# A two-layer decoder on one core: new order of the turn, with a ring of 12 decays

## What is computed

```python
x = ln(x + rfs(x) @ weights.T)                 # 1 random features: exp(x@proj - |x|^2/2 ...)
x = ln(x + xattn(x, ctx, ctx))                 # 2 cross attention, 16 heads of 16, 120 keys
x = ln(x + coupling(x))                        # 3 three cycles of a 4-layer gelu network and a rotation
x = ln(x + mamba(x))                           # 4 below
x = ln(x + gated(x, ctx, ctx, ctx))            # 5 gelu(x@ctx.T) * (x@ctx.T) @ ctx
x = ln(x + moe(x))                             # 6 router, 8 experts, the best one weighted by its gate

def coupling(x):                               # 3
    g = global_net(x.mean(rows)); out = x
    for _ in range(3):
        t = sigmoid(w4 @ gelu(w3 @ gelu(w2 @ gelu(w1 @ out))))
        out = out + (0.1 + range * (0.7*g + 0.3*t - 0.5) * 2) * twist(out)
    return out

def mamba(x):                                  # 4
    xs, res = split(x @ W_in.T)                # 512 + 512 columns
    xc = silu(conv4(xs) + b)
    delta = softplus(xc)
    for n in range(16):                        # 16 states per column
        h[n] = scan(h[n] * exp(-delta * exp(A_log[n])) + xc*xc)
    return ((sum(h) * silu(res) + D) * xc) @ W_out.T
```

## Time and profile before

| | |
|---|---|
| device time, median of 3 runs | 3486.57 us |
| the profiled execution: its time, its span | 3486.94 us, 3485.1 us |
| mean granted TensorE clock | 0.814 of full |
| PE, PE weight load busy | 76%, 43% of the span |
| DVE busy | 76% |
| ACT, POOL busy | 45%, 46% |
| DMA | 13 GB/s mean |

### The profile page before, as it was taken

One profiled execution on the slowest core, in us unless ns is written; L12 is line 12 of the kernel. 1 busy time (PEld: TensorE's weight loads), 2 busy tenths in 40 slices (PEclk: granted clock), 3 DMA queues, 4 the chain that ended last, 5 costly groups with the idle time before them and its releaser, 6 DMA issues.

```text
span 3485.1 us, 41835 instructions
## 1 busy us (share of the span) xinstructions
PE 2634.2 (76%) x10956; PEld 1505.0 (43%) x10956; DVE 2650.8 (76%) x4314; ACT 1564.4 (45%) x2838; POOL 1610.6 (46%) x1223
## 2 busy tenths in 40 slices
PE   5876878787786887768787786877778787777746
PEld 3434435354443544435354443544445353443413
DVE  2287887968789687887968789696877968788693
ACT  1364544535345453544535445453544545354430
POOL 1064461735537263562735437262562726447180
PEclk8868788887888878888887888888788887888877
DMA  3000000000000000000000000000000000000000
GB/s 115 0 16 0 21 1 27 0 22 6 0 27 0 27 0 7 21 0 27 0 22 6 0 27 0 27 0 13 15 0 27 0 22 6 0 12 0 12 0 12
DMA packets 16786, 45.63 MB, mean 13 GB/s; under 512 B 2376, under 2 KB 6992, under 8 KB 16336
## 3 DMA queue, kind: packets, MB, share of 16 engines
q1 hardware_dynamic: 16592, 43.90, 3.5%
HBM read 35.50 MB, written 8.39 MB: 13 GB/s over the span
## 4 chain that ended last, share of the span: by engine, by line
PE 37%; DVE 28%; issue 19%; ACT 9%; POOL 4%; DVEq 2%; SPq 0%; DMA 0%; ACTq 0%; POOLq 0%
PE bank L487 35%; DVE h_ring L1010 10%; POOL ysum L1537 4%; DVE x L392 3%; DVE x L1107 2%; PE bank L400 2%; DVE smax L915 2%; DVE soft L990 2%; ACT a_ring L1372 1%; DVE ln_stats L374 1%; DVE xpad L1016 1%; ACT soft L1349 1%; DVE qT L965 1%; ACT bank L1367 1%; ACT kmask L1312 1%
## 5 line engine op out<-in xcount | busy, mean ns | idle before, releaser
L1537 POOL TENSOR_TENSOR ysum<-ysum,h_ring 128x512 f32<-128x512 f32 x896 | 1152.4, 1286 | 476.5 <-DVE h_ring L1010 411.2
L1010 DVE TENSOR_TENSOR_SCAN h_ring<-a_ring,bank 128x512 f32<-128x512 f32 x1024 | 1170.9, 1199 | 103.2 <-ACT a_ring L1372 50.8
L487 PE MATMUL bank<-w_expert_w,x45T 128*128 128x512 f32 x1024 | 607.8, 732 | 226.2 <-DVE x L1107 224.6
L1372 ACT ACTIVATE a_ring<-soft,decay 128x510 f32<-128x510 f32 x1024 | 666.7, 715 | 141.7 <-DVE h_ring L1010 140.2
L1513 POOL TENSOR_TENSOR kmask<-kT,w_columns 128x960 f32<-128x960 f32 x64 | 115.5, 1838 | 753.8 <-ACT kT L1260 753.8
L487 PEld LDWEIGHTS bank<-w_expert_w,x45T 128*128 128x128 f32 x1024 | 212.3, 224 | 501.4 <-DVE x L1107 276.2
L1282 ACT ACTIVATE probs<-bank 120x512 f32<-120x512 f32 x256 | 138.3, 593 | 411.8 <-PE bank L487 411.8
L487 PE MATMUL bank<-kmask,w_cn_w 128*128 128x256 f32 (+2 forms) x768 | 277.3, 470 | 44.1 <-ACT kmask L1316 20.3
L400 PE MATMUL bank<-w_ident,x 128*128 128x128 f32 x640 | 136.8, 350 | 224.9 <-DVE x L392 224.9
L1107 DVE SCALAR_TENSOR_TENSOR x<-bank,weight,x 128x256 f32<-128x256 f32 x512 | 212.0, 471 | 72.0 <-PE bank L487 72.0
L962 DVE TENSOR_SCALAR kmask<-kmask,gate_scale,base 128x256 f32<-128x256 f32 x96 | 40.3, 420 | 278.7 <-ACT kmask L1326 278.7
(11 more groups left out here) (144 smaller groups left out, 3879.8 us busy)
## 6 DMA issues: line engine op xcount, KB each, us to landing
x0T<-in_xT SPq DMA_DIRECT2D x16, 512.0 KB, 3.2
x<-in_x SPq DMA_DIRECT2D x16, 512.0 KB, 4.2
out<-x SPq DMA_DIRECT2D x16, 512.0 KB, 3.1
ctxT<-in_ctxT SPq DMA_DIRECT2D x16, 240.0 KB, 4.3
ctxTb<-in_ctxT SPq DMA_DIRECT2D x16, 240.0 KB, 2.6
ctxb<-in_ctx SPq DMA_DIRECT2D x16, 240.0 KB, 3.1
w_expert_w<-in_expert_w SPq DMA_DIRECT2D x1, 2048.0 KB
w_winT<-in_winT SPq DMA_DIRECT2D x1, 1024.0 KB
```

The source lines that it names most:

```text
L487: return pe.matmul(o, l, r, start=start, stop=stop)
L1010: scanned.then(v.tensor_tensor_scan(h_ring[:, k % HRING, :], a_ring[:, k % RING, :, :].rearrange("p b s -> p (b s)"), xc2, 0.0, ALU.mult, ...
L1372: a.activation(a_ring[:, k % RING, :, 1:S], delta[:, c, :].rearrange("p (b s) -> p b s", b=NB)[:, :, 1:S], ACT.Exp, scale=decay[:, k:k + 1 ...
L1537: p.tensor_tensor(out=total, in0=first, in1=h_ring[:, k % HRING, :], op=ALU.add)\
```

## The change

The computation is the same. What changes is the order of a turn and what goes with it:

- RING is 12. `BEFORE_COUPLING` is step 54 of the plan, after scan 51. All steps from there (12 scans and an out) are done on DVE between the rotations, two scans per cycle; the last out follows the cycles. ACT still ends all decays before the first gelu of the cycles, so that decay 63 waits for scan 51. On DVE all 54 steps, and then `global_base`, stand ahead of the scans that are left.
- The output projection of m (`mamba_out`) and its layer norm (`ln4_sum`) move out of the cycles into the head of the next turn, where the group is b. ACT keeps a copy of its residual (`keep`).
- `mamba_in` 0 to 3 moves up in the head, before the projection of f; `mamba_in` 4 to 7 moves out of the head to between the attention's scores, all into bank 4, each waiting for ACT to have read the one before. ACT loads the silu table once more for it.
- `convolve`, silu and softplus are cut in halves, and DVE does the norm of f between them.
- Keys and values of the next group are made in cycles 1 and 2. Keys are masked by ACT (4 activations with a scale of 0 or 1 per partition); POOL's `mask_keys` is gone, and tiles that lay in kmask get their own memory.
- `combine` and `experts` steps, maxima and the softmax steps of ACT get new places: expert 13 comes after the transposes of norm 2 on PE, experts 14 and 15 in cycles 1 and 2.
- POOL squares the next group's input (`norms`) before its additions of chunk 3.

```diff
-RING = 8
+RING = 12
+BEFORE_COUPLING = AFTER["scan", (IC * STATES - RING - 1) // STATES, (IC * STATES - RING - 1) % STATES]
...
 # PE, turn
                 if b is not None:
-                    norm_turn(pe, n4, b, MB)
+                    mamba_out(b, 0, 8)
+                if m is not None:
+                    norm_turn(pe, n3, m, TURN)
+                if b is not None:
+                    mamba_out(b, 8, 16)
+                if m is not None:
+                    mamba_in(m, f, 0, IC)
...
                     project(f, n1, feats_ready, feats, rf_out, DC, OUT12)
                 if b is not None:
+                    norm_turn(pe, n4, b, MB)
                     gated_in(b)
...
+                    norm_turn(pe, n1, f, TURN)
+                    queries(f)
+                    scores(f, 0, 2)
+                if b is not None:
+                    gated_out(b)
+                if f is not None:
+                    scores(f, 2, 3)
+                if b is not None:
+                    norm_turn(pe, n5, b, MB)
+                if f is not None:
+                    scores(f, 3, 4)
+                if b is not None:
+                    router(b)
+                if f is not None:
+                    scores(f, 4, 5)
+                if b is not None:
+                    turn_weights(b)
                 if m is not None:
+                    mamba_in(m, f, IC, IC + 1)
                 if b is not None:
                     expert_bias(b)
+                for j in range(3):
+                    if f is not None:
+                        scores(f, 5 + j, 6 + j)
+                    if m is not None:
+                        mamba_in(m, f, IC + 1 + j, IC + 2 + j)
...
-                    experts(b, 12, 14)
+                    experts(b, 12, 13)
                 if f is not None:
                     norm_turn(pe, n2, f, TURN)
                 if b is not None:
-                    experts(b, 14, 15)
+                    experts(b, 13, 14)
                 if f is not None:
                     layer(f, 1, 0)
...
                 for s in range(CYC):
...
-                    out = 4 * (s - 1) if m is not None and 1 <= s < 5 else None
-                    if out is not None:
-                        mamba_out(m, b, out, out + 2)
+                    if s == 1 and nxt is not None:
+                        keys(nxt, f)
+                    if s == 2 and nxt is not None:
+                        values(nxt, f)
                     if f is not None:
                         layer(f, 2, s)
-                    if out is not None:
-                        mamba_out(m, b, out + 2, out + 4)
+                    if b is not None and s in (1, 2):
+                        experts(b, 13 + s, 14 + s)
                     if f is not None:
                         layer(f, 3, s)
 # DVE, turn_
+                if b is not None:
+                    ln4_sum(b)
+                    norm_apply(v, n4, b)
+                if m is not None:
+                    convolve(m, 0)
                 if f is not None:
                     ln1_sum(f)
                     norm_apply(v, n1, f)
+                if m is not None:
+                    convolve(m, 2)
                 if b is not None:
                     gated(b)
                 if f is not None:
-                    values(f)
...
+                    maxima(f, 0, 2)
                 if b is not None:
                     ln5_sum(b)
                     norm_apply(v, n5, b)
                 states(m, 1)
...
-                states(m, 52)
+                states(m, 46)
                 if f is not None:
                     ln2_sum(f)
-                states(m, 53)
+                states(m, 47)
                 if f is not None:
                     norm_apply(v, n2, f)
                 if b is not None:
                     combine(b, 12, 14)
-                states(m, 58)
-                if b is not None:
-                    combine(b, 14, 16)
-                states(m, len(PLAN) - 1)
+                states(m, BEFORE_COUPLING)
                 if f is not None:
                     global_base(f)
                 for s in range(CYC):
+                    states(m, BEFORE_COUPLING + 3 + 2 * s)
                     if f is not None:
                         rotate(f, s)
-                    if s == 0:
-                        states(m, len(PLAN))
-                    if b is not None and s == 3:
+                    if nxt is not None and s == 1:
+                        values(nxt)
+                    if b is not None and s == 2:
+                        combine(b, 14, 16)
+                    if b is not None and s == 4:
                         ln6_stats(b)
-                    if m is not None and s == CYC - 2:
-                        ln4_sum(m)
-                if m is not None:
-                    norm_apply(v, n4, m)
+                states(m, len(PLAN))
 # ACT, turn_
+                    silu()
+                    silu_conv(m, 0, 2)
                 if f is not None:
                     norm_copy(a, n1, f, TURN)
...
+                    silu_conv(m, 2, IC)
+                if f is not None:
+                    queries(f)
+                if b is not None:
+                    gated(b)
                 nat()
                 if m is not None:
-                    softplus(m)
+                    softplus(m, 0, 2)
+                decays(m, 4)
                 if b is not None:
                     norm_rstd(a, n5, b)
                     norm_copy(a, n5, b, MB)
+                if m is not None:
+                    softplus(m, 2, IC)
...
+                decays(m, 12)
+                if m is not None:
+                    silu()
+                    mamba_in(m, IC, 2 * IC)
+                    nat()
-                for k, ahead in enumerate((11, 15, 21, 25, 29, 31, 38, 42)):
+                for k, ahead in enumerate((12, 16, 20, 24, 28, 31, 36, 40)):
...
+                if m is not None:
+                    keep(m, b)
+                decays(m, 50)
+                if f is not None:
+                    norm_rstd(a, n2, f)
                 decays(m, 54)
-                if f is not None:
-                    norm_rstd(a, n2, f)
-                decays(m, 56)
                 if f is not None:
                     copy_and_sum(f)
                 decays(m, STEPS)
 # POOL
-            def mask_keys(g):
...
+                    if c == IC - 1 and nxt is not None:
+                        norms(nxt)
```

More of the change, by code:

```diff
@@ L415, in program @@
         MB = [bank[6], bank[7]]
+        IN = [bank[4 + j % 2 if j < IC else 4][:, :] for j in range(2 * IC)]
         def added_after(s):
@@ L825, in turn @@
                     layer(f, 1, 1)
-                if b is not None:
-                    experts(b, 15, 16)
-                if f is not None:
                     glob(f, 2)
@@ L1461, in turn_ @@
                         network(f, 2, s)
+                        if nxt is not None and s == 1:
+                            keys(nxt)
                         network(f, 3, s)
```

316 lines of the change are left out of this document (152 added, 164 removed).

## The result

The changed kernel takes 3505.3 us (median of 10 executions, 3496.4 to 3508.1), the kernel before, on the same chip, 3484.2 (3482.4 to 3490.0). The ratio is 1.0056, with a 95% interval of 1.0046 to 1.0065: slower by 0.6%. The profiled execution took 3505.96, its span is 3504.1. The forecast was 3534, slower by 1.4%: the sign is right, the size isn't, and the rest of this text shows that the reason given for the sign didn't hold either.

What follows compares the result with a forecast made beforehand. No engine is near full, so waits between engines bound the turn. Six stretches sum to 211.5 us, 3.1 more than 208.4; over fifteen turns + 47 gives 3534 us. Forecast's own range 3494 to 3590 (0.45), overall range 3400 to 3630.

Steps and rivals of the forecast that it cites:

- expert 13 cold behind the transposes: On PE behind norm 2's transposes: expert 13 takes 3.6 us if PE is cold, and DVE's combine waits for it.
- VectorE idle for 8.0 us ahead of `base`: On DVE before the rotations: `global_base` stands ahead of the remaining scans, so DVE idles for about 9 us.
- the copies 11.3 us behind the apply: On ACT: `copy_and_sum` comes some 10 us behind the apply of norm 2, not right behind.
- the first rotation gap: Rotation 0 to rotation 1 in the cycles: 8 to 10 us, not 13.5.
- X to R: End of norm 2's apply to rotation 0's first instruction: 23.5 us before, forecast 27.5.
- R to E: The cycles, rotation 0's first instruction to rotation 5's end: 38.5 us before, forecast 39.0, range 35.7 to 45.
- E to L: The head, from rotation 5's end (E) to the routing logits: 54.8 us before, forecast 55.7, between 54.5 and 57.
- W to C: Experts' weights to DVE's copy of the attention's maxima: 15.9 us before, forecast 20.5, from 18 to 24.
- A granted clock near 1: PE between the experts' weights and the copy of the attention's maxima: a sign that the forecast is wrong.
- C to X: Copy of the attention's maxima to end of norm 2's apply: 71.5 us before, forecast 64.7, between 63.5 and 66.
- the first and the last turns: Program's ends: keys and values ahead of turn 0, same last out; counted at 0, within 8 us either way.
- clock stays high: Rival: inner projections and keys keep PE at 2.4 GHz; turn 203.2 us, whole 3409, from 3380 to 3480; chance 0.37.

Runs made afterwards that it cites:

- e2: Changed kernel with expert step 13 on PE ahead of norm 2's transposes instead of behind them: 3444.4 us, ratio 0.9892.
- e1: Changed kernel with ScalarE's copies of norm 2's transposes moved ahead of the last chunk's square and its decays: 3511.7 us, ratio 1.0084.
- e3: Changed kernel with seven steps (six scans, one output) ahead of VectorE's wait for the global base, one scan per coupling cycle: 3493.8 us, ratio 1.0022.
- e8: Changed kernel with the matmuls of inner projections 4 to 7 over 64 of 512 columns, waits and order kept: 3471.2 us, ratio 0.9956.
- e6: Changed kernel with two unread VectorE reductions ahead of rotation 5, 1.2 us more work per turn: 3484.7 us, ratio 1.0006.
- e4: Changed kernel with all thirteen steps (twelve scans, an output) ahead of the global base and none in the cycles: 3547.1 us, ratio 1.0175.
- e7: Changed kernel with four unread VectorE reductions ahead of rotation 5, 2.4 us more work per turn: 3469.3 us, ratio 0.9953.
- e14: Changed kernel with one unread VectorE reduction ahead of rotation 5, 0.6 us more work per turn: 3479.2 us, ratio 0.9988.
- e5: Changed kernel with the edits of e1, e2 and e3 together: 3425.1 us, ratio 0.9828. Its theory 1: the turn's period comes in steps 3.4 us apart.
- e12: e5 with inner 4 ahead of norm 5 and, in the last states-only turn, inner 4 to 7 in the head: 3404.9 us, ratio 0.9771.

## Why the prediction was right and wrong

**The mechanisms of the sum.** Those of the coupling are shown by rows: expert 13 cold behind the transposes (3.62, forecast 3.6), VectorE idle for 8.0 us ahead of `base` (forecast about 9), the copies 11.3 us behind the apply (forecast some 10), the first rotation gap down from 13.5 to 9.9 us, rotations with instructions of over 1 us. e2 shows the chain (X to R from 28.6 to 23.0), e1 that the copies only ride on it, and e3 that scans beside the rotations cost time there: R to E from 40.3 to 35.5, its clock rising from 0.95 to 1.00 in the same windows, so not all of the 4.8 is VectorE's.

**The mis-sized terms.** *E to L* was 55.7 and is 53.5. I had the second half of the convolution begin 28.8 us behind E, which it does (28.6), and end at 35.5, with 1.9 for POOL's bias step beside it; it ends at 33.5, and the 1.9 is the error. Behind it lies a misread row: the prediction put the 6.16 us of the first six steps down to `mask_keys`, but the mask ended at 1404.80 and the six began at 1405.00; what ran beside them was the bias step (last section). The mask slowed the two steps ahead of them, to 1.95 and 2.01 us, where such a step takes 0.48. *W to C* was 20.5 and is 18.1: a range of 18 to 24 stood in the text, and I took a middle that no turn had. With the four projections whole and in their place, every full turn of the ten traces that have them so goes by this: where the first takes 2.8 to 3.6 us and the second 2.0, W to C is 17.4 to 18.2; where both are cold (3.6 and 3.8), it is 21.4 to 21.9. And the stretch isn't 15.9 plus what the projections cost: PE spends 4.3 us in them in e8 and 8.8 in e6, and it is 17.5 in both. A granted clock near 1 there was named as a sign that the prediction is wrong; it is 0.86, where it was 0.58. *X to R* (27.5, is 28.6) and *R to E* (39.0, is 40.3) were short by 1.1 and 1.3.

**The step that failed** is "211.5, 3.1 more than 208.4. Fifteen turns: + 47". The errors of the parts are -2.2 (E to L), -2.4 (W to C), -1.1 (C to X), +1.1 and +1.3, together -3.3 us per turn, and the measured turn is 208.2 as before: the twelve turns in the middle cost 0.1 us, not 37. All fifteen cost 10.3, nearly all of it in turns 1 and 15.

Under it lies a step that I didn't see as one: that what is added or saved in one stretch is added to or saved from the turn. e1, e3 and e4 saved 1.3, 7.1 and 3.7 us in the stretches that they edit, and the turn moved by 0, 0 and +3.4. With work added it moved by -3.4 and by +6.8. What changes in step with it is where PE's granted clock stands at 0.50 and where at 1, in stretches with equal instructions. The prediction held the clock as a thing of each stretch, with a rival in which it is high everywhere. The runs show it as a thing of the whole turn: an edit in one stretch moves the rise of the clock in another, in which nothing was edited (e1, e3).

**The edges** are all of the difference in this execution, 19 us. What the prediction called the first and the last turns (turn 0 and what follows the last rotation) it counted at nothing, within 8; they are +2.3 and +6.4. Turn 1 (+7.1) and turn 15 (+4.5) stood among its fifteen. Parts of the 19 have a cause in the order of the work. In turn 1 there are no experts, and X to R is 22.7 in place of 15.5: ScalarE waits for a scan ahead of its square and then makes twelve decays ahead of the gelu table, where it made eight without a wait. The table is loaded 12.8 us behind X, and was 7.2 behind. In the drain the gate half stands between decay 12 and the rest. ScalarE, after, past the last rotation:

```profile
3316.04 1.28 ACT L1360 ACT_TABLE_LOAD   x1
3321.57 0.60 ACT L1357 ACTIVATE res<-bank 128x512 f32<-128x512 f32 x1 [3.64 <-PE bank L491]
3328.82 4.99 ACT L1402 ACTIVATE a_ring<-soft,decay 128x510 f32<-128x510 f32 x8
```

From 3316.04 to 3328.82 no decay is made: 12.8 us. The 13th scan starts 34.0 us behind the first, in the kernel before 23.8. Of that 10.2, 4.1 are given back by the earlier first scan; the 6.1 that are left are nearly all of the 6.4. What follows the last rotation is 238 to 241 us in all runs on the changed kernel with this order of the drain. On the kernel before it is 233.6, and 235.9 to 239.3 with work added (0.6 to 3.6 us of that is the added work itself, which runs once there too). Turn 15 (+4.5) and some of turn 1 go with the clock: in e3 turn 15 takes 201.8 and turn 1 175.9 with the code of those turns changed only in the coupling. For the 2.3 of turn 0 no run gives a cause.

**Was it right to say slower?** By the measurement, yes, and by luck: the 3.1 us per turn that the sum went by didn't come, and the 19 us that came in their place lie at the ends of the program, for reasons that aren't in the sum. With work added to both, the changed kernel is faster at two amounts of four, slower at one, and the same within the noise at one. The rival "clock stays high", at 203.2 us per turn, is what e6, e7 and e14 came near to, at 204.4 to 204.8 in their short turns. The range of 3400 to 3630 was so wide that it holds the medians of all sixteen experiments (3405 to 3580), whatever their edit.

**What stays open:** why the turns settle where they do. In eleven of the changed and tried kernels nearly all full turns have one of 201.4, 208.2, 211.6 and 215.0 us; in the six others they go between two or more lengths (and the kernel before stays within 207.9 to 208.4). Theory 1 of e5 had something: with the 204.8 of e7 these lengths lie on steps 3.4 us apart. And where lengths alternate, their mean does so by simple fractions: 203.1 in e5 is halfway between 201.4 and 204.8, 206.5 in e8 and in e14 halfway between 204.8 and 208.2, and the three turns of e6 have a mean of 205.9, a third of the way. With such steps 1.2 us can be lost and the next 1.2 cost 3.4 per turn, as on the kernel before; why there are steps, no run shows. That a difference in work smaller than a step can be lost, doubled or turned round is measured; that PE's clock is what closes the loop is supported by the equal instructions at unequal durations, and wasn't tried by holding the clock.

## What to carry to other kernels

In a loop like this one, in which an engine's granted clock falls and rises within the turn, a change of a few us per turn can't be judged by one build: put known delays into both versions, on the path, and compare the pairs. Here five pairs gave -74 to +39 us for one change of 0.6%. What paid here were savings of several us in a stretch with idle engines (expert 13 into PE's idle 6.2 us, the scans into VectorE's idle 8.0), judged in their own stretch and kept together: 1.1% in e2, 1.7% in e5, 2.3% in e12. These are single builds too; that the gain holds with delays added wasn't tried. And count the first and last turns: the gate half is hidden behind attention in a full turn, and isn't in a turn that has none.

## What the runs showed of the hardware that I had not expected

**More work, less time.** 2.4 us more per turn made the changed kernel 36 us faster, and seven eighths less of the gate half for PE (e8) gave the same W to C as the whole of it (e6), 17.5, as PE stood at its low level for longer. A 128x512 projection of four matmuls is 1.98 us or 3.62 to 3.78 in adjacent places of one stretch.

**Who pays when VectorE and POOL run side by side.** I had let the convolution pay, as the rotation does (0.42 alone, 1.44 beside POOL). In the head, after, it is POOL that pays: its bias step ran beside the six steps of the second half of the convolution and took 6.08 us; in turn 0, which has no convolution, it takes 2.35. The six steps took the 4.06 that they take alone. POOL, then VectorE:

```profile
1418.06 6.08 POOL L1551 TENSOR_TENSOR x<-x,w_rows 128x1024 f32<-128x1024 f32 x1 [30.69 <-PE bank L403]
```
```profile
1417.86 4.06 DVE L1005 SCALAR_TENSOR_TENSOR soft<-xpad,w_columns,soft 128x512 f32<-128x512 f32 x6
```

The kernel before has the same pair with the roles turned, beside the first of the six steps that took 6.16 us from 1405.00:

```profile
1404.93 2.36 POOL L1518 TENSOR_TENSOR x<-x,w_rows 128x1024 f32<-128x1024 f32 x1
```

POOL's step took its 2.36 us, and the one step of VectorE that began 0.07 us behind it took 2.84 where the others take 0.74. So it is, within 0.6 us, in all fifteen turns of either kernel that have the pair. In either kernel the engine that began first went on at its usual pace and the other waited: after, VectorE's steps followed each other without a gap from 1417.86 to 1421.92, and POOL's, begun at 1418.06, ended 2.2 us behind the last of them. (Starts and ends on POOL are rough.)

The Trainium skill, in the GPSIMD Engine Reference, Specifications, has the two engines share their interfaces to SBUF; the trace agrees that they slow each other, and adds that it is not always the same one that waits. That the order of the starts decides is read from these two orders; no run changed the order alone.
